# A four-layer graph network: count blocks with one node a step instead of a pair, built in groups of eight steps

## The reference, cut to what matters

```python
x = _layernorm(x + mlp(x, edge_attr_32, src, dst))      # relu([x_src, x_dst, e] @ W1 + b1) @ W2 + b2, summed by dst
x = _layernorm(x + gatv2(x, edge_index, edge_attr_16))  # 4 heads, softmax over each destination's edges
x = _layernorm(x + gat(x, edge_index))                  # 1 head, softmax over each destination's edges
gathered = xs[src]                                      # the last layer, "mean":
sums = segment_sum(gathered, dst); counts = segment_sum(ones, dst)
x = _layernorm(x + sums / maximum(counts, 1.0)[:, None])
```

## Time and profile before

| what | value |
|---|---|
| time before, median of 3 runs | 8260.32 us (8241.33 to 8264.79) |
| span of the profiled execution, first to last instruction | 6975.1 us |
| busy: PE, DVE, ACT, POOL | 5545.7, 4763.3, 1449.0, 4949.6 us |
| mean TensorE clock that was granted | 0.563 of full speed |
| DMA | 995.18 MB in 1384856 packets |
| device time of the profiled execution itself | not given apart; the span is all that is known of it |

### The profile page before, as it was taken

How to read it: one execution, slowest core, us unless ns; L and a number is a source line. 1 busy time by engine, 2 the same in 40 slices (tenths; PEclk the granted TensorE clock), 3 DMA queues, 4 the chain that set the end, 5 groups by cost and what they waited for, 6 DMA issues and landing times. The chain is left out here.

```text
span 6975.1 us, 134144 instructions
## 1 busy us (share of the span) xinstructions
PE 5545.7 (80%) x36891; PEld 4916.1 (70%) x36891; DVE 4763.3 (68%) x7973; ACT 1449.0 (21%) x4328; POOL 4949.6 (71%) x5209
## 2 busy tenths in 40 slices
PE   5897888777776778888778885588888888888399
PEld 4676777666665666666666663588888888887399
DVE  4557777777755788888888875566666666666455
ACT  1112222222212222222222221222222222222200
POOL 4777777777775777777777776377777777777444
PEclk6556555666665555555555555555555555555599
DMA  6756666666653555555555553554545555554397
GB/s 158 180 144 155 159 159 159 159 158 160 159 149 87 152 146 146 146 145 146 145 146 145 146 146 80 63 112 110 110 110 110 110 110 110 110 110 95 117 360 292
DMA packets 1384856, 995.18 MB, mean 143 GB/s; under 512 B 927331, under 2 KB 1293029, under 8 KB 1375046
## 3 DMA queue, kind: packets, MB, share of 16 engines
q1 hardware_dynamic: 906390, 750.00, 36.6%
q0 software_dynamic: 165856, 169.99, 14.7%
q10 hardware_dynamic: 312400, 72.71, 5.1%
HBM read 676.85 MB, written 315.92 MB: 142 GB/s over the span
## 5 line engine op out<-in xcount | busy, mean ns | idle before, releaser
L469 POOL DMA_INDIRECT gat_G<-gat_src,src_cols x1612 | 1530.2, 949 | 592.8 <-issue 490.3
L469 POOL DMA_INDIRECT mlp_G<-mlp_src,src_cols x1612 | 1533.4, 951 | 533.5 <-issue 487.2
L469 POOL DMA_INDIRECT gatv_G<-gatv_src,src_cols x1612 | 1527.5, 948 | 524.8 <-issue 491.0
L810 PE MATMUL gat_z<-gat_win,gat_hot 128*128 128x1 f32 x3234 | 721.0, 352 | 274.4 <-DVE gat_msg L552 212.9
L810 PEld LDWEIGHTS gat_z<-gat_win,gat_hot 128*128 128x128 f32 x3234 | 707.3, 330 | 318.8 <-issue 279.7
L806 PE MATMUL gatv_z<-attr_w,gatv_attrT 112*128 112x448 f32 x462 | 425.1, 1024 | 408.6 <-DVE gatv_msg L552 398.8
L846 PE MATMUL gat_sums<-gat_msg,gat_same 128*128 128x65 f32 x3234 | 713.6, 410 | 0.0
L846 PEld LDWEIGHTS gat_sums<-gat_msg,gat_same 128*128 128x128 f32 x3234 | 708.2, 330 | 0.0
L846 PE MATMUL gatv_sums<-gatv_msg,gatv_same 128*128 128x68 f32 x3234 | 689.6, 403 | 0.0
L846 PEld LDWEIGHTS gatv_sums<-gatv_msg,gatv_same 128*128 128x128 f32 x3234 | 687.3, 321 | 0.1
L846 PE MATMUL mlp_sums<-mlp_act_out,mlp_same 128*128 128x64 f32 x3234 | 632.7, 374 | 0.0
(11 more groups left out here) (494 smaller groups left out, 10679.4 us busy)
## 6 DMA issues: line engine op xcount, KB each, us to landing
mean_block<-blocks SPq DMA_DIRECT2D x74, 1568.0 KB, 10.1
sums_gatv<-gatv_out_rows SPq DMA_DIRECT2D x231, 252.0 KB
sums_gat<-gat_out_rows SPq DMA_DIRECT2D x231, 231.0 KB, 2.4
blocks<-gat_build_area SPq DMA_DIRECT2D x216, 245.0 KB
mlp_rel<-rel_rows SPq DMA_DIRECT2D x231, 224.0 KB
sums_mlp<-mlp_out_rows SPq DMA_DIRECT2D x231, 224.0 KB
gatv_rel<-rel_rows SPq DMA_DIRECT2D x231, 224.0 KB
gat_rel<-rel_rows SPq DMA_DIRECT2D x231, 224.0 KB
```

What stands on the lines that cost most here:

```text
L469: pool.indirect_dma_start(out=G[:, b.gq, j * L.gathered:(j + 1) * L.gathered], out_offset=None, in_=L.gather_table, in_offset=bass.Indirec ...
L810: last = pe.matmul(z[b.q % 2][:, j * w:(j + 1) * w], hot[:, b.q, j, :], win[:, b.q, j, part * w:(part + 1) * w], start=not ax and part == ...
```

## The change

A step now belongs to a tile and **one** destination node: 7936 steps in 62 halves of 128 steps, with 49 keys each instead of 98. Steps are built eight at a time (an *octet*), two octets a batch, in batches 48 to 199 of mlp, 8 to 199 of gatv2 and 48 to 199 of gat (304, 384 and 304 octets). The one-hots of an octet are laid out with two steps innermost, so that the innermost dimension of every operand has two neighbouring bf16 values; `one_hots` of mlp and gatv2 and the histogram's `count` are written in that way too. The octets gather in an SBUF half (`halves`, the areas of `masks` and `work`), and SP stores a whole half of 1568 KB every eighth batch. The weights of the mean layer's matmuls lie side by side. ACT's first act in a step is now to copy the last octet of the batch two before. The loop body has 16 batches. The numbers of the steps are worked out in five portions. In mlp `same` has two buffers instead of four and the relu is done in place.

```diff
-U = 8
+U = 16
-PAIRS = N // 2
-NS = ETILES + PAIRS - 1
-SB = NS // P
-KEYS = 2 * HI
+SB = -(-(ETILES + N - 1) // P)
+NS = SB * P
-BUILD = {"mlp": (48, PASS_C, 9, 0), "gatv2": (0, PASS_C, 5, 1512), "gat": (0, PASS_C, 10, 2592)}
+K2, OCTET = 2, 8
+HALF_OCTETS = P // OCTET
+HALF_W = HI * P
+BUILD = {"mlp": (48, 200, 2, 0), "gatv2": (8, 200, 2, 304), "gat": (48, 200, 2, 688)}
...
-        same = sb("same", [P, Q, B, P])
+        SQ = Q if soft else 2
+        same = sb("same", [P, SQ, B, P])
...
-                o = i + (-2)
+                o = i + (-3)
                 if o.exists() and builds(o):
-                    wait(sp, blocks_copied, built(o))
-                    sp.dma_start(S["blocks"][:, bass.ds(first_of(o) * KEYS, per_batch * KEYS)],
-                                 block_out[:, o.c % 2, :]).then_inc(blocks_out[o.c % 2], 16)
+                    k, loops = half_of(o, per_batch)
+                    if k % HALF_OCTETS == 0:
+                        h = k // HALF_OCTETS - 1
+                        wait(sp, blocks_copied, octet(o, per_batch))
+                        sp.dma_start(S["blocks"][:, bass.ds((loops + (h + first_octet // HALF_OCTETS)) * HALF_W, HALF_W)],
+                                     halves[h % 2].rearrange("p h e -> p (h e)")).then_inc(blocks_out[h % 2], 16)
...
-                nc.vector.tensor_tensor(hot[:, b.q, :, :], relv[:, b.q, :, :],
-                                        bc(lane_of, 2, [P, B, P]), ALU.is_equal).then_inc(hot_made, 1)
+                if L.win_dt == BF16:
+                    nc.vector.tensor_tensor(
+                        hot[:, b.q, :, :].rearrange("p b (a e) -> p (b a) e", e=D // 2),
+                        rel[:, b.q, :].rearrange("p (b e) -> p b e", e=D // 2), bc(lanes_of, 1, [P, 4 * B, D // 2]),
+                        ALU.is_equal
+                    ).then_inc(hot_made, 1)
...
-            def build_hots(b):
-                wait(dve, blocks_made, built(b, back=2))
-                cols = bass.ds(first_of(b), per_batch)
-                nc.vector.tensor_tensor(hot_src[:, b.c % 2, :, :], bc(iota_of, 1, [P, per_batch, P]),
-                                        bc(S["src_lo"][:, cols], 2, [P, per_batch, P]), ALU.is_equal)
+            def build_hots(b, k):
+                wait(dve, blocks_made, octet(b, k + 1 - ring))
+                cols = bass.ds((octet(b, k) + first_octet) * OCTET, OCTET)
+                for hot_of, of_step, w in ((hot_src, S["src_lo"], P), (hot_key, S["keys"], HI)):
+                    last = nc.vector.tensor_tensor(
+                        hot_of[:, slot(b, k), :, :, :], bc(steps2_of[:, 0:w, :], 1, [P, OCTET // K2, w, K2]),
+                        bc(of_step[:, cols].rearrange("p (g k) -> p g k", k=K2), 2, [P, OCTET // K2, w, K2]), ALU.is_equal)
+                last.then_inc(hots_made, 1)
...
+            def copy_octet(b, k):
+                wait(act, blocks_made, octet(b, k + 1))
+                at, loops = half_of(b, k)
+                h, e = at // HALF_OCTETS, at % HALF_OCTETS * OCTET
+                if e == 0:
...
+                    if h >= 2:
+                        wait(act, blocks_out[h % 2], (loops // 2 + h // 2) * 16)
+                act.activation(halves[h % 2][:, :, e:e + OCTET], build_of, ACT.Copy).then_inc(blocks_copied, 1)
...
+                if d.exists() and builds(d):
+                    copy_octet(d, per_batch - 1)
+                if soft and d.exists():
+                    exponentiate(d)
                 if L.window and i.exists():
                     nonlinear(i)
+                if p.exists() and builds(p):
+                    copy_octet(p, 0)
...
+            def build_octet(b, k):
+                wait(pe, hots_made, octet(b, k + 1))
+                wait(pe, blocks_copied, octet(b, k))
+                for e in range(OCTET):
+                    g, j = e // K2, e % K2
+                    last = pe.matmul(build_of[:, :, e], hot_src[:, slot(b, k), g, :, j], hot_key[:, slot(b, k), g, :, j],
+                                     start=True, stop=True)
...
-            for c, (s, n) in enumerate(MEAN_HALVES):
-                j, k = c // 2, c % 2 * MSTEPS
-                pe.wait_ge(block_in[2 * (j % SLOTS) + c % 2], 16 * (j // SLOTS + 1))
+            for c in range(H):
+                pe.wait_ge(block_in[c % SLOTS], 16 * (c // SLOTS + 1))
                 wait(pe, parts_added, c - 1)
-                counts = block[:, j % SLOTS, k * KEYS:(k + n) * KEYS].rearrange("p (e h) -> p h e", h=HI)
+                counts = block[:, c % SLOTS, :, :]
```

More of the change, by code:

```diff
@@ L275, in edge_pass @@
         masks = masks[:, :, :, :].rearrange("p r a e -> p (r a e)")
-        area = build_area[:, :].bitcast(F32)
+        halves = [whole.bitcast(BF16)[:, 0:HALF_W].rearrange("p (h e) -> p h e", e=P) for whole in (masks, work)]
         M = L.msg
@@ L456, in _ @@
             for q in range(2):
-                sp.wait_ge(blocks_out[q], 16 * len(range(build_from + q, build_end, 2)))
+                wait(sp, blocks_out[q], halves_stored(q))
             if hist:
@@ L503, in add_gathered @@
                 if not soft:
-                    wait(dve, act_done, b.used(Q))
+                    wait(dve, sums_made, b.used(Q))
                 w = L.window
@@ L589, in step @@
                 if i.exists() and builds(i):
-                    build_hots(i)
+                    for k in range(per_batch):
+                        build_hots(i, k)
                 if soft and (i + 2).exists():
@@ L611, in carry_tails @@
                     dve.wait_ge(turns_copied, len(turns))
-                    dve.wait_ge(blocks_copied, block_count)
-                    for q in range(2):
-                        dve.wait_ge(blocks_out[q], 16 * len(range(build_from + q, build_end, 2)))
+                    wait(dve, blocks_made, block_count)
                     v.memset(top[:, 0:1], 0.0)
@@ L845, in make_sums @@
                         rhs = Gv[:, b.gq, j, :]
-                    last = pe.matmul(sums[b.q % 2][:, j * L.msg:(j + 1) * L.msg], same[:, b.q, j, :], rhs,
+                    last = pe.matmul(sums[b.q % 2][:, j * L.msg:(j + 1) * L.msg], same[:, b.c % SQ, j, :], rhs,
                                      start=True, stop=True)
@@ L1880, in _ @@
                     centre(c)
[L1882 to L1885 removed]
+SLOTS = 5
 OLD_Q = 4
 FAR = 1024.0
[L1888 to L1890 removed]
 PARTS_OF = [(0, 7), (7, 14), (21, 14), (35, 14)]
 W = D + 1
[L1893 removed]
+assert sum(m for _, m in PARTS_OF) == KN
+IN_MASKS, IN_STEPS = RB * 2, NS // 2 // P
 def step_parts(S):
[L1898 to L1900 removed]
+    masks = S["masks"][:, :, :, :].rearrange("p r a e -> p (r a e)")
+    parts, first = [], 0
+    for area, halves in ((masks, IN_MASKS), (S["keys"][:, :].bitcast(F32), IN_STEPS),
+                         (S["src_lo"][:, :].bitcast(F32), IN_STEPS)):
+        n = min(halves * P, NS - first)
+        parts.append((area[:, 0:n], first, n))
+        first += n
+    assert first == NS
+    return parts
 def mean_layer(nc, L, S, out):
[L1905 removed]
+    H = SB
     ctx = ExitStack()
@@ L2034, in _ @@
                                 pe.wait_ge(lessened, 2 * (i + 1))
-                    last = pe.matmul(y[c % 2][0:w, 0:3 * W], counts[:, h, :], parts[:, h, :], start=h == 0,
+                    last = pe.matmul(y[c % 2][:, 0:3 * W], counts[:, h, :], parts[:, h, :], start=h == 0,
                                      stop=h == KN - 1)
```

401 lines of the change are left out of this document (179 added, 222 removed).

## The result

In the first comparison the changed kernel took 8531.2 us (median of 4 runs, 8503.5 to 8558.1) against 8256.4 us before: a ratio of 1.0329, 95% interval [1.0301, 1.0357]. It is slower; 8198 us and "faster" were forecast.

What follows compares the result with a forecast made beforehand. POOL's gathers at 1.25 us each were taken to bound the passes, PE the mean layer. The terms -56 - 4 - 1 - 3 + 2 = -62 us gave 8260 - 62 = 8198 us, range 8165 to 8280.

Steps and rivals of the forecast that it cites:

- Fewer halves: Mean layer on PE: 74 halves become 62, at 4.67 us each, 56.0 us less.
- pace: Mean layer on PE: weights lying side by side make each half 0.07 us shorter, 4 us less in all.
- `twice`: Mean layer: this copy goes from ahead of the first matmul, 0.9 us less.
- DVE's one-hots: Soft passes and mlp: comparisons run at double rate, 1024 elements in 0.68 us; gatv2's batch +0.14 us, covered.
- Rivals 1 and 3: DVE comparisons stay at single rate, 8290 us, chance 0.15; or faster ones keep POOL out, 8680 us or more, 0.03.
- PE: the step that failed: Octet matmuls on PE: two octets cost 1.0 us against 0.6 in gatv2, +0.4 us, within its 1.73 us wait.
- something in the new order that no row shows: Anywhere in the new order of work: an effect not seen in the profile, no size given, chance 0.03.
- ACT and its order: gatv2: exponentials behind the last octet's copy cost nothing to 0.5 us a batch, under POOL's slack.
- The rest at nothing: Gat's start gives back 3 us; step numbers, 16-batch loop code and dense parts were taken to cost nothing.
- SP's bursts: Whole-half stores of 1568 KB delay gathers in gatv2 and gat: 2 us taken, ends 0 and 77 us.
- rival 2: Whole-half stores hold up POOL's gathers: 8273 us at the bound, 8234 at half of it, chance 0.09.
- Rival 4: Mean layer speeds up fully: -82 us, stretched by 1.18 to -97, 8163 us, chance 0.04.

Runs made afterwards that it cites:

- after_again: The changed kernel without edit, run and profiled again beside the kernel before: 7074.1 against 6974.7 us, ratio 1.0148.

## Why the prediction was wrong

**The footing.** "The timed median is 1285 us above the span, and I leave those as they are" took two executions at different levels for one. The profiled execution of the kernel before takes its span and 2 us. The reasons could be tested only at the level of 6975 us, and there too the sign was wrong: +96 to +99 us against -62.

**Fewer halves, pace, `twice`.** Right: -56 - 4 - 1 = -61 forecast, -58.3 measured behind gat's last gather. The pace gave 0.02 us a half instead of 0.07.

**DVE's one-hots.** Right, within 0.02 us each for the steps and `hot`, and hidden; every second `count` of mlp stayed at the single rate, hidden too. The double rate holds with one operand in PSUM in the others. So the row of the Trainium skill's "VectorE: DVE Perf Modes", section "The perf-mode tier table", that speaks of one element a cycle with a PSUM operand did not hold for this comparison, and section 5.1 of "Vector Engine (DVE) Microarchitecture Reference" agrees with the trace there; for every second `count`, which meets the conditions that the prediction took from it, it does not. Rivals 1 and 3 fell with it: gathers kept their 0.948 us.

**PE: the step that failed.** "+0.4 us, within its 1.73 us. The first octet runs where PE waits for the messages." Three things were wrong in it. The price was: the prediction put an octet's matmul at no more than the 0.063 us of a 64-column one, and at the 1.2 GHz level it took 0.10 (0.81 over 8), so two octets cost +1.05 us in gatv2 in place of +0.4, and +0.65 in gat. Why it is dearer than one with more columns no run shows. The cover was taken from gatv2 and not looked up in gat, where it was 1.02 us. And above all the wait for the bank was not priced: a first octet can't start until ACT has copied the last one, which is the last thing PE did, so PE stands still for 0.68 us in nearly every built batch however much slack ACT has (137.1 us in the 192 of gatv2, 101.6 in the 152 of gat). With the octets' price this used up the cover: 9.04 us a batch in gat, and 9.10 in gatv2 at the low clock, in place of 8.74. The chance left for "something in the new order that no row shows" was 0.03.

**ACT and its order.** "Cost nothing to 0.5 us in the batch, under POOL's slack." The place was right and the slack was not, since the exponentials lead to the messages, `z` and POOL: in gatv2 at 2760 us this path is the one that ends last. Neither order alone explains the loss: mending ACT's left gatv2 as it was, mending PE's made gat worse, and both together gave back 98 of the 118 us of the soft passes.

**The rest at nothing.** Code of 16 batches: right (0.9999). The start of gat: the 3 us did not come back; POOL's longest wait there is 4.4 us against 4.0. The numbers of the steps: wrong, 27 to 36 us in mlp. I looked at DVE's portions; the cost was PE's and ACT's, 62 groups in 17 of the batches 11 to 45, up to four one behind the other.

**SP's bursts.** Taken at 2 us, bounds 0 and 77. Storing in quarters shortened gatv2 by 8 us and left gat alone, so the term was somewhat small; rival 2 was not what happened. The stores that were replaced numbered 600 (168, 216 and 216), not 552; nothing hangs on it.

**Rival 4** (the mean layer at its full gain) did not happen.

## What to carry to other kernels

When one buffer is shared by the last instruction of a step and the first of the next on the same engine, the round trip to the engine that empties it stops the first engine in each step (here 0.68 us a batch), so price it before looking for slack. Read the cover of every engine in every stage and at the clock of that stage: 1.7 us in one pass said nothing of the 1.0 us in the next. And see that the profiled execution and the timed ones are at one level before reasoning on the difference.

## What the runs showed that was not expected

In the first comparison a kernel took 8256 us that took 6972 to 6983 us in all later ones. The first profile of the changed kernel is from there. In it the mean layer runs as elsewhere, 4.65 us a half, and a gather is 0.948 us, but a batch of gat that builds nothing takes 10.2 us in the middle in place of 8.74, and one that builds 10.4. Work that waits for PE starts late. The first profile has this pair,

```profile
4009.43 0.86 PE L900 MATMUL gatv_build_ps<-gatv_hots 128*128 128x49 bf16 x8
...
4011.63 0.50 ACT L759 ACTIVATE masks<-gatv_build_ps 128x392 bf16<-128x392 f32 x1 [3.78 <-PE gatv_build_ps L900]
```

1.34 us from the recorded end to the copy, against 0.03 us at 5098.95 above. Over all copies ahead of which ACT had been idle for more than 1 us the middle is 2.7 us in mlp and 2.9 in gatv2 and gat, and 0.04 us in after_again, worked out from the rows of both traces. Also SP's register moves for the window loads, 29 ns each, took up to 1398 ns there (min, median and max of the tile `gat_win`; first that profile, then after_again):

```profile
L167 SPq MOVE gat_win<-gat_dst x924: 2/29/1398, 5653.9 to 8066.3; - x185
```

```profile
L167 SPq MOVE gat_win<-gat_dst x924: 29/29/38, 4538.0 to 6602.1; - x185
```

That the change costs 275 us there and 96 to 99 us elsewhere fits with its additional handovers from PE to ACT and back, but no run shows it: no experiment met that level, and what makes results of PE late on it stays open.
